# A decoder layer on one core: the quantised cross-product stage and the late weight splits rewritten

## What is computed

```python
x = x + attn(layernorm(x))       # 32 heads of 128, RMS norm on q and k, softmax, all heads through Wo
x = x + matmul(fq(layernorm(x), s1, z1), fq(ctx, s2, z2))
x = x + ffn(layernorm(x))        # x @ base_W.T + base_b, and 8 gated low-rank experts

def fq(x, s, z):
    q = clip(round(x / s + z), 0, 255)
    return (q - z) * s
```

## Time and profile before

| | us |
|---|---|
| median of 3 runs (lowest to highest) | 538.18 (537.94 to 539.28) |
| the profiled execution | 540.05 |
| its span, first to last instruction | 537.7 |
| granted TensorE clock, mean | 1.000 |
| busy: PE, PEld, DVE, ACT, POOL | 523.5, 462.0, 331.1, 355.9, 271.6 |
| chain that ended last | PE 90%, DVE 5%, ACT 2%, DMA 1%, issue 1%, POOL 1% |

### The profile page before, as it was taken

One profiled execution on the slowest core, in us unless ns is written; L12 is line 12 of the kernel. 1 busy time (PEld: TensorE's weight loads), 2 busy tenths in 40 slices (PEclk: granted clock), 3 DMA queues, 4 the chain that ended last, 5 costly groups with the idle time before them and its releaser, 6 DMA issues.

```text
span 537.7 us, 9702 instructions
## 1 busy us (share of the span) xinstructions
PE 523.5 (97%) x3198; PEld 462.0 (86%) x3198; DVE 331.1 (62%) x695; ACT 355.9 (66%) x745; POOL 271.6 (51%) x229
## 2 busy tenths in 40 slices
PE   6999999999999999999999999999999999999887
PEld 6888888888888888999999999999999999986475
DVE  6254444266666677666666666666666666676755
ACT  3566666556666767777777677767767776775740
POOL 3344444365454445554646455464646556465340
PEclk9999999999999999999999999999999999999999
DMA  5344635323332221112122111211142311220002
GB/s 182 126 139 134 230 96 174 89 89 98 94 100 83 74 81 55 47 57 60 59 59 59 57 43 56 59 59 59 59 121 62 126 50 60 60 78 21 2 0 79
DMA packets 23350, 43.41 MB, mean 81 GB/s; under 512 B 3616, under 2 KB 3616, under 8 KB 23072
## 3 DMA queue, kind: packets, MB, share of 16 engines
q1 hardware_dynamic: 23328, 43.13, 26.3%
HBM read 41.03 MB, written 2.10 MB: 80 GB/s over the span
## 4 chain that ended last, share of the span: by engine, by line
PE 90%; DVE 5%; ACT 2%; DMA 1%; issue 1%; POOL 1%; SPq 0%; DVEq 0%
PE p_t L483 5%; PE p_v L562 5%; PE p_v L564 5%; PE p_o L483 5%; PE p_t L484 5%; PE p_o L484 5%; PE p_v L563 5%; PE p_o L486 5%; PE p_t L486 5%; PE acc L581 5%; PE acc L582 5%; PE acc L583 5%; PE p_t L548 5%; PE p_o L600 3%; PE p_o L602 3%; PE p_o L601 3%
## 5 line engine op out<-in xcount | busy, mean ns | idle before, releaser
L1078 DVE TENSOR_TENSOR w_lo<-raw,w_hi 128x512 fp32r<-128x512 f32 x64 | 44.2, 690 | 78.0 <-ACT w_hi L693 78.0
L945 POOL TENSOR_TENSOR wo_lo<-raw,wo_hi 128x512 fp32r<-128x512 f32 x31 | 40.1, 1294 | 100.4 <-ACT wo_hi L827 100.4
L693 ACT CAST w_hi<-raw 128x512 fp32r<-128x512 f32 x64 | 39.9, 623 | 67.5 <-PE p_t L486 30.3
L762 ACT ACTIVATE probs<-p_s,nbias,rq_t 128x256 f32<-128x256 f32 x128 | 71.3, 562 | 19.1 <-DVE nbias L1180 19.1
L562 PE MATMUL p_v<-w_hi,xnt_hi 128*128 128x256 f32 x256 | 77.2, 301 | 0.0
L564 PE MATMUL p_v<-w_hi,xnt_lo 128*128 128x256 f32 x256 | 72.3, 282 | 0.0
L563 PE MATMUL p_v<-w_lo,xnt_hi 128*128 128x256 f32 x256 | 72.2, 282 | 0.0
L927 POOL TENSOR_TENSOR acc_k<-acc_k,square 128x512 f32<-128x512 f32 x32 | 41.7, 1304 | 53.3 <-ACT square L708 53.3
L927 POOL TENSOR_TENSOR acc_q<-acc_q,square 128x512 f32<-128x512 f32 x32 | 43.5, 1361 | 40.2 <-ACT square L708 39.9
L811 ACT CAST pt_hi<-p_t 128x512 fp32r<-128x512 f32 x64 | 37.4, 584 | 38.8 <-PE p_t L548 38.8
L945 POOL TENSOR_TENSOR w_lo<-raw,w_hi 128x512 fp32r<-128x512 f32 x32 | 44.9, 1403 | 20.5 <-ACT w_hi L745 20.5
(11 more groups left out here) (263 smaller groups left out, 1483.7 us busy)
## 6 DMA issues: line engine op xcount, KB each, us to landing
raw<-in_wv SPq DMA_DIRECT2D x36, 256.0 KB, 2.6
raw<-in_wk SPq DMA_DIRECT2D x32, 256.0 KB, 2.6
raw<-in_wq SPq DMA_DIRECT2D x32, 256.0 KB, 2.6
raw<-in_wo SPq DMA_DIRECT2D x31, 256.0 KB, 2.6
ctx_f<-in_ctx SPq DMA_DIRECT2D x4, 512.0 KB, 3.6
xin<-in_x SPq DMA_DIRECT2D x4, 256.0 KB, 3.5
xb<-in_x SPq DMA_DIRECT2D x4, 256.0 KB, 6.0
ctx_kept<-ctx_k SPq DMA_DIRECT2D x1, 1024.0 KB, 5.0
```

Of the source, the lines that this page charges most:

```text
L762: act.activation(probs[:, b, a, :], p_s[:, a, :], ACT.Exp, bias=nbias[:, b, a:a + 1], scale=rq_t[:, 2 * b + a:2 * b + a + 1], accum_out=rs ...
L945: pool.tensor_tensor(dst, raw[:, slot, :], hi, ALU.subtract).then_inc(w_lo_pool, 1)
L1078: dve.tensor_tensor(w_lo[:, n, 0:NC * DH], raw[:, r, :], w_hi[:, n, 0:NC * DH], ALU.subtract).then_inc(w_lo_dve, 1)
```

## The change

Five parts.

1. **One-step quantiser.** linear clips at 0 itself (Relu), quantise is one VectorE operation (min with 255, add 12582912), the transposes are of fp32 xn, and q1_out takes away 12582912 + 128 by a bias while it writes bf16.
2. **Scaling inside the residual sum.** scaled is gone. ScalarE copies x1 from the accumulator to x_res (keep_x1); second_sum multiplies the product by s1 s2 and adds x_res in one operation.
3. **Row part in the last sum.** The 16 one-column matmuls come together (row_sums, between the first two transposes of x3), row_part makes rsd with the constant once, and the final sum adds it.
4. **Split column part.** corr becomes corr_hi (ScalarE) and corr_lo (VectorE, column_lo), added by two fp32r matmuls a tile in place of the fp32 one.
5. **Late splits three pairs forward.** The casts and low parts of ra, bm and wo_last move into slots 0, 1 and 2 of pair 13; mark_experts moves to the end of pair 14; the load of wo_last_f moves from before the last pair's loads to pair 10.

```diff
         def add_column_part(pe, t):
+            if t % 2 == 0:
+                pe.wait_ge(col_lo_done, t // 2 + 1)
             pe.wait_ge(linear_done, t + 1)
-            pe.matmul(acc[t][:], ident[:], corr[:, t // 2, :], start=False, stop=True, skip_group_check=True)
+            pe.matmul(acc[t][:], ident_r[:], corr_hi[:, t // 2, :], start=False, stop=False, skip_group_check=True)
+            pe.matmul(acc[t][:], ident_r[:], corr_lo[:, t // 2, :], start=False, stop=True, skip_group_check=True
+                      ).then_inc(col_part_added, 1)
...
         def transpose_q1(pe, t):
             pe.wait_ge(q1_done, t + 1)
             if t >= 2:
-                pe.wait_ge(scaled_done, t - 1)
+                pe.wait_ge(q1t_out, t - 1)
...
         def quant_product(pe, t):
             pe.wait_ge(q1t_out, t + 1)
+            if t >= 2:
+                pe.wait_ge(x2_done, t - 1)
+            elif t == 1:
+                pe.wait_ge(col_lo_done, 2)
...
             def linear(t):
                 act.wait_ge(coef_ready, t // 2 + 1)
-                act.activation(xn[:, t, :], acc[t][:], ACT.Identity, scale=cs[:, t:t + 1], bias=cb[:, t:t + 1]
+                act.activation(xn[:, t, :], acc[t][:], ACT.Relu, scale=cs[:, t:t + 1], bias=cb[:, t:t + 1]
                                ).then_inc(linear_done, 1)
+            def keep_x1(t):
+                act.wait_ge(col_part_added, t + 1)
+                act.copy(x_res[:, t, :], acc[t][:]).then_inc(x1_kept, 1)
             def q1_out(t):
                 act.wait_ge(q1t_ready, t + 1)
-                act.copy(q1t[:, t, :, :].rearrange("p c n -> p (c n)"), p_flat[2 + t % 2].bitcast(BF16)[:, 0:D]
-                         ).then_inc(q1t_out, 1)
+                act.activation(q1t[:, t, :, :].rearrange("p c n -> p (c n)"), p_flat[2 + t % 2], ACT.Identity,
+                               bias=qc[:, 7:8]).then_inc(q1t_out, 1)
...
+            def quantise(t):
+                dve.wait_ge(linear_done, t + 1)
+                dve.tensor_scalar(xn[:, t, :], xn[:, t, :], QMAX, ROUND, ALU.min, ALU.add).then_inc(q1_done, 1)
             def second_sum(t):
-                dve.wait_ge(scaled_done, t + 1)
-                dve.tensor_tensor(x_res[:, t, :], acc[t][:], xn[:, t, :], ALU.add).then_inc(x2_done, 1)
+                dve.wait_ge(x1_kept, t + 1)
+                dve.wait_ge(product_ready, t + 1)
+                dve.scalar_tensor_tensor(out=x_res[:, t, :], in0=p_flat[t % 2], scalar=qc[:, 2:3],
+                                         in1=x_res[:, t, :], op0=ALU.mult, op1=ALU.add).then_inc(x2_done, 1)
...
+                    if peeled(p, NP - 3, NP - 2):
+                        last_weights_lo(j)
+                    if peeled(p, NP - 2, NP - 1) and j == 3:
+                        mark_experts()
...
-                dve.tensor_tensor(xn[:, t, :], p_flat[t], x_res[:, t, :], ALU.add).then_inc(out_done, 1)
+                dve.scalar_tensor_tensor(out=xn[:, t, :], in0=p_flat[t], scalar=rsd[:, t:t + 1],
+                                         in1=x_res[:, t, :], op0=ALU.add, op1=ALU.add).then_inc(out_done, 1)
```

More of the change, by code:

```diff
@@ L97, in decoder_layer @@
         ident_r = here("ident_r", [P, P], F32R)
-        ident_b = here("ident_b", [P, P], BF16)
         ones = here("ones", [P, P], F32)
@@ L783, in column_part @@
                 act.wait_ge(col_sums_ready, b + 1)
-                act.activation(corr[:, b, :], p_flat[1 + b], ACT.Identity, scale=qc[:, 3:4], bias=qc[:, 6:7]
+                act.activation(corr_hi[:, b, :], p_flat[2 - b], ACT.Copy, scale=qc[:, 3:4]
                                ).then_inc(col_part_done, 1)
@@ L817, in pair @@
                         v_half_hi(p + 1, j // 2, 1 - par)
-                    if last and j == 0:
-                        act.wait_ge(wo_last_landed, 16)
-                        act.copy(wo_last_hi[:], wo_last_f[:]).then_inc(wo_last_hi_done, 1)
                     if last and j == 3:
@@ L829, in pair @@
                         pair_weights_hi(0, par, j // 2, 3 + 2 * p + j // 2)
+                    if peeled(p, NP - 3, NP - 2):
+                        if j == 0:
+                            act.wait_ge(ra_landed, 16)
+                            act.copy(ra_hi[:], ra_f[:]).then_inc(rab_hi_done, 1)
+                        elif j == 1:
+                            act.wait_ge(bm_landed, 16)
+                            act.copy(bm_hi[:], bm_f[:]).then_inc(rab_hi_done, 1)
+                        elif j == 2:
+                            act.wait_ge(wo_last_landed, 16)
+                            act.copy(wo_last_hi[:], wo_last_f[:]).then_inc(wo_last_hi_done, 1)
             pair(0, 0)
@@ L837, in _ @@
             pair(NP - 1, 1, last=True)
-            act.wait_ge(ra_landed, 16)
-            act.copy(ra_hi[:], ra_f[:]).then_inc(rab_hi_done, 1)
-            act.wait_ge(bm_landed, 16)
-            act.copy(bm_hi[:], bm_f[:]).then_inc(rab_hi_done, 1)
             last_out_hi(1)
@@ L876, in x3_hi @@
                          ).then_inc(x3_hi_done, 1)
-            for t in (0, 1):
-                linear(t)
-            for t in (0, 1):
-                q1_out(t)
-            for t in (2, 3):
-                linear(t)
-            for t in (0, 1):
-                scaled(t)
-            for t in (2, 3):
-                q1_out(t)
+            linear(0)
+            linear(1)
+            keep_x1(0)
+            keep_x1(1)
+            q1_out(0)
+            q1_out(1)
+            linear(2)
+            linear(3)
+            keep_x1(2)
+            q1_out(2)
+            q1_out(3)
             normalise(0)
-            scaled(2)
+            keep_x1(3)
             x3_hi(0)
             normalise(1)
-            scaled(3)
             x3_hi(1)
@@ L967, in mark_experts, with last_weights_lo @@
                 ins.then_inc(experts_marked, 1)
-            def split_low_rank():
-                pool.wait_ge(rab_hi_done, 1)
-                pool.tensor_tensor(ra_lo[:], ra_f[:], ra_hi[:], ALU.subtract).then_inc(rab_lo_done, 1)
-                pool.wait_ge(rab_hi_done, 2)
-                pool.tensor_tensor(bm_lo[:], bm_f[:], bm_hi[:], ALU.subtract).then_inc(rab_lo_done, 1)
+            def last_weights_lo(j):
+                if j == 0:
+                    pool.wait_ge(rab_hi_done, 1)
+                    pool.tensor_tensor(ra_lo[:], ra_f[:], ra_hi[:], ALU.subtract).then_inc(rab_lo_done, 1)
+                elif j == 1:
+                    pool.wait_ge(rab_hi_done, 2)
+                    pool.tensor_tensor(bm_lo[:], bm_f[:], bm_hi[:], ALU.subtract).then_inc(rab_lo_done, 1)
+                elif j == 2:
+                    pool.wait_ge(wo_last_hi_done, 1)
+                    pool.tensor_tensor(wo_last_lo[:], wo_last_f[:], wo_last_hi[:], ALU.subtract
+                                       ).then_inc(wo_last_done, 1)
             def pair(p, par, last=False):
@@ L981, in pair @@
                     if last and j == 3:
-                        split_low_rank()
                         break
-                    if last and j == 2:
-                        pool.wait_ge(wo_last_hi_done, 1)
-                        pool.tensor_tensor(wo_last_lo[:], wo_last_f[:], wo_last_hi[:], ALU.subtract
-                                           ).then_inc(wo_last_done, 1)
                     if j % 2:
@@ L1007, in _ @@
                                    ).then_inc(rstd_ready, 1)
-            mark_experts()
             for t in range(NT):
@@ L1330, in _ @@
             pair_variance(0, n)
+            column_lo(0)
             pair_coefficients(0)
@@ L1334, in _ @@
             quantise(0)
+            quantise(1)
             pair_coefficients(1)
+            column_lo(1)
+            second_sum(0)
             quantise(2)
-            second_sum(0)
             n0 = stats3(0)
+            quantise(3)
+            variance3(0, n0)
             second_sum(1)
-            variance3(0, n0)
+            bias3(0)
             n1 = stats3(1)
-            bias3(0)
             variance3(1, n1)
+            second_sum(2)
             bias3(1)
-            second_sum(2)
             x3_lo(0)
             n2 = stats3(2)
+            second_sum(3)
+            variance3(2, n2)
             x3_lo(1)
-            variance3(2, n2)
-            second_sum(3)
             n3 = stats3(3)
```

75 lines of the change are left out of this document (37 added, 38 removed).

## The result

| | before | changed |
|---|---|---|
| median of 22 runs each (lowest to highest) | 539.11 (537.94 to 541.50) | 540.96 (539.74 to 542.44) |
| the profiled execution | 540.05 | 541.12 |
| its span | 537.7 | 539.0 |
| mean granted TensorE clock of it | 1.000 | 0.996 |

The ratio is **1.0027** (95% interval 1.0017 to 1.0037): slower by 0.17% to 0.37%, small, but clear of no change. A second set of 12 runs of the same changed kernel gave 541.20, ratio 1.0031 (1.0010 to 1.0052).

The account below looks back on a forecast made before the run. TensorE was taken to bound the pairs before the last, a chain across ScalarE, VectorE and TensorE the stage. Pair 13 +0.9, last pair +1.7, stage and tail -1.9 make +0.7, median 538.9, range 536.5 to 540.8.

Parts of the forecast that it names:

- Within 0.3%: Whole kernel: the case of at most 1.6 either way, given chance 0.65, against faster 0.15 and slower 0.20.
- The stage, -1.7: Last stage: shorter links from the first column part bring the second transposes of x3 1.7 earlier, at 510.6 for 512.29.
- Router and last sum, -0.19: Behind the stage: router's product clear of GpSimd's last sums gives back 0.25; last sum with a scalar costs 0.06.
- Pair 13, +0.9: Pair 13: bm_lo ahead of k_lo and q_lo delays the scores 0.74, and held nbias adds some 0.2.
- slack 0.52, so TensorE waits 0.74: Pair 13, scores of head 28: q_lo comes 1.26 late against a slack of 0.52, so TensorE waits 0.74.
- nbias and the scaling stretched by more than 1 with TensorE waiting for probabilities: Pair 13: a listed sign that the forecast is wrong, stretches of more than 1 on VectorE.
- The forecast's share for ra_lo, 0.2: Pair 13: ra_lo holds nbias about 1.2, so wo_hi and bm_lo come some 0.2 later, on the same wait.
- Last pair, +1.7: Last pair: marks before k_lo and q_lo delay the scores of head 31 by 2.2; freed nbias gives back 0.5.
- The sum by the page of the Trainium skill: Whole kernel: the exclusive port lock holds k_lo of head 31 for 0.5, making +1.2 in place of +0.7.
- that the late splits are absorbed: Rival, last pair: GpSimd's nine small operations take about 0.5 for 2.5; -1.8, at 536.4; chance 0.15.
- That GpSimd and VectorE block each other: Rival: moved subtractions block VectorE; 1.6 in pair 13, 2.7 in last pair, stage -1.6; +2.7, 540.9; chance 0.15.
- The stage did not shrink less: Rival, stage: copies cost 0.7 and a sum waits for one, so it gives 1.0; +1.6, at 539.8; chance 0.10.

Follow-up runs that it names:

- e2: Changed kernel with all of part 5 undone (splits, marks, casts and DMA where they were), so parts 1 to 4 alone: 537.31, ratio 0.9968.
- e11: e5 with the two-step quantiser again (Identity for Relu, one VectorE pass more per tile): 540.06, one execution; stage 16.40 against 14.68.
- e12: e5 with one fp32 matmul per tile for the column part in place of two fp32r: 536.66, one execution; stage 15.95 against 14.68.
- e8: Changed kernel with ra's split and the marks put back, wo_last and bm still split in pair 13: 537.12, one execution.
- e1: Changed kernel with mark_experts back behind the second rstd in the stage, the three splits staying in pair 13: 537.86, ratio 0.9985.
- e4: Kernel before the change with part 5 alone added: 543.12, ratio 1.0081.
- e6: The changed kernel run again, nothing altered: 541.20, ratio 1.0031.
- e9: e5 with the cast and all eight mark comparisons again before k_lo of head 31: 541.30, ratio 1.0031.
- e3: Changed kernel with ten filler matmuls, result unread, before the scores of head 31 to keep TensorE busy: 541.23, ratio 1.0043.
- e5: Changed kernel with ra, bm and the marks put back, only wo_last still split early in pair 13: 536.24, ratio 0.9933.
- e7: Changed kernel with the ten filler matmuls once more, beside the changed kernel on one chip: 541.29, ratio 1.0031.
- e10: e5 with the cast and four of the eight mark comparisons before k_lo of head 31: 538.12, ratio 0.9981.

## Why the prediction was right, and where not

The forecast was 538.9 for a before of 538.18, 0.13% up; measured is 0.27% up (0.17 to 0.37). Within 0.3% was the right case, and the direction inside it too, at about half of the measured size. The measured median 540.96 stands beside a before of 539.11 in the same set, 0.9 above the one shown ahead, so the ratio is what is compared: on 538.18 it gives 539.6, inside the range of 536.5 to 540.8. Part of the agreement is luck. Two costs are missing from the sum, 0.75 in pair 13 and 1.4 of lower clock in the profiled executions. By the stretches the profiled execution is 2.66 longer, 0.49%, outside the case; it is the medians that lie inside, and no run settles how they come to 0.27%.

- **The stage, -1.7**: right, -1.74, link by link, and independent of the rest (e2). e11 and e12 show that the chain runs through all four quantiser passes and all four column parts, which is more than the forecast's sum has on it.
- **Router and last sum, -0.19**: -0.33; TensorE waits 0.18 for 0.41.
- **Pair 13, +0.9**: the mechanism was right and the size short, +1.65. The step that failed is "slack 0.52, so TensorE waits 0.74" as the only wait. The first wait is 0.87 with its delays; the second, of TensorE for the scaled probabilities, adds the rest. The forecast named that term and kept it out of the sum, because no row showed a one-input VectorE operation inside a subtraction. Now rows do: 1.08 and 1.37, 1.12 and 1.36, for 0.35 alone. In all the traces together, from 425 on, 22 scalings start inside a subtraction; they take 1.08 to 1.39, and each ends 0.14 to 0.16 behind it. The Trainium skill's rule (SBUF — State Buffer, section SBUF: two separate sides), that the shared port pair is locked for the whole instruction and that VectorE's fast modes take it too, agrees with them. The forecast had named this as a sign of being wrong, nbias and the scaling stretched by more than 1 with TensorE waiting for probabilities, and it came: 1.22 for 0.16, 1.37 for 0.35, a wait of 0.47. The forecast's share for ra_lo, 0.2, is the 0.21 between e8 and the changed kernel.
- **Last pair, +1.7**: in two parts. Wait and give-back were right: scores +2.28 (forecast 2.2), back 0.58 in e1 (forecast 0.5); without the clock the stretch is +1.7, as forecast. What no part of the prediction has is the granted clock: 1.4 up to the next scores in every profile with that wait (changed, e4, e6, e9; 4.91 to 4.93 for 3.54), and at this place in no profile without it (e1, e2, e3, e5, e7, e8, e10, e11, e12).
- **The sum**: by the trace's stretches +1.3 without the lower clock and +2.66 with it. The sum by the page of the Trainium skill was +1.2, but by another term, k_lo of head 31 held for 0.5; k_lo took 1.39 for 1.30. At full clock the spans are 1.6 (and 1.4 in e6) above before, the medians 1.5 to 2.0 above.
- **The rivals**: that the late splits are absorbed fell with the waits. That GpSimd and VectorE block each other came true in part: its 1.6 for pair 13 is near what was measured (1.65), while its price for the last pair did not come this way, and rstd did not slow the stage. The stage did not shrink less.

Left open: e4 at full clock is 4.6 above before, where its stretches without the lower clock add up to 3.3; for the changed kernel it is 1.6 and 1.4 against 1.3. The start alone moves the profiled executions by up to 1.7 (the fifth w_lo from 20.13 to 21.85, with the clock at 1.00), and e4 has only four executions at full clock, so this may be chance. The mean clock may also hide short low stretches; no trace of such an execution is at hand. How much of the medians is the lower clock also stays open: it comes in 22 of 34 executions of the changed kernel, against 26 of 71 before.

## What to carry to other kernels

Before work is moved forward on a queue, read who waits for what stands behind it: nine operations of 15 elements, 0.20 to 0.28 each, hidden where they were, cost the last pair 3.66 in the trace, 2.28 of it the wait and 1.4 the lower clock behind it. A change in halves that do not touch each other can be summed by stretches, and the half that loses be taken back: e5 is 0.67% faster than before, while the whole change is 0.27% slower. Where a GpSimd subtraction is moved beside VectorE's work on SBUF, count the products and scalings there whose tensors all lie in SBUF (nbias and the scaling of the probabilities here) as ending with the subtraction (0.01 to 0.16 behind it), not with their own time, and look for the second wait that follows. Operations that read a bank, and the reciprocal of two columns, were not held.
